# Attention on one core: sixteen 64 KB block moves a step become four of 256 KB, and the key projections read their tokens in another order

## The reference

```python
h = _layernorm(x, ln1_g, ln1_b)
x = _attention(h, h, sa_wq, sa_wk, sa_wv, sa_wo, sa_bo) + x
h = _layernorm(x, ln2_g, ln2_b)
x = _attention(h, cond_emb, ca_wq, ca_wk, ca_wv, ca_wo, ca_bo) + x
h = _layernorm(x, ln3_g, ln3_b)
p = h @ ff_w1 + ff_b1
a, gate = (p[..., :D_FF], p[..., D_FF:])
h = a * jax.nn.gelu(gate, approximate=False) @ ff_w2 + ff_b2
return h + x
```

## Time and profile before

| | |
|---|---|
| median of 3 runs | 2921.08 us (2920.36 to 2922.96) |
| the profiled execution, its own time | 2921.73 us |
| span of its trace | 2919.9 us |
| busy: PE, DVE, ACT, POOL | 2874.1, 2279.7, 1906.4, 1470.9 us |
| TensorE clock granted, mean | 0.998 |
| DMA packets | 535597, 413.62 MB |
| self-attention, cross-attention, feed-forward | up to about 1203, 2371, 2920 us |

### The profile page before, as it was taken

How to read it: one execution, slowest core, us unless ns; L and a number is a source line. 1 busy time by engine, 2 the same in 40 slices (tenths; PEclk the granted TensorE clock), 3 DMA queues, 4 the chain that set the end, 5 groups by cost and what they waited for, 6 DMA issues and landing times.

```text
span 2919.9 us, 75820 instructions
## 1 busy us (share of the span) xinstructions
PE 2874.1 (98%) x25278; PEld 2506.6 (86%) x25278; DVE 2279.7 (78%) x3495; ACT 1906.4 (65%) x6041; POOL 1470.9 (50%) x1310
## 2 busy tenths in 40 slices
PE   8999999999999999999999999999999999999999
PEld 6888888888888888877788888888888889999999
DVE  6888888888888888888888888888888865555554
ACT  6666676776666667876677777777777754444443
POOL 5444444444444444754555555555555545454454
PEclk9999999999999999999999999999999999999999
DMA  5555565555555555556666666666665532222222
GB/s 146 152 158 157 159 158 156 156 157 149 150 149 149 146 149 151 152 157 164 160 168 172 169 167 160 162 160 160 164 160 160 154 107 72 90 72 75 87 72 62
DMA packets 535597, 413.62 MB, mean 142 GB/s; under 512 B 171200, under 2 KB 520768, under 8 KB 535488
## 3 DMA queue, kind: packets, MB, share of 16 engines
q1 hardware_dynamic: 443424, 328.31, 41.4%
q10 hardware_dynamic: 92064, 83.96, 11.3%
HBM read 94.52 MB, written 49.02 MB: 49 GB/s over the span
## 4 chain that ended last, share of the span: by engine, by line
PE 59%; SPq 12%; ACT 11%; DVE 7%; issue 5%; ACTq 3%; DMA 1%; POOL 1%; DVEq 0%; POOLq 0%
PE unit_ps L594 32%; PE s_ps L594 12%; SPq L524 11%; PE o_ps L619 8%; PE s_ps L607 7%; ACT probs L851 7%; DVE neg_max L1031 2%; DVE blocks L1045 2%; ACTq L867 2%; ACT qk_hi L889 2%; DMA rows_in<-rows_t_dram 1%; DVE hT_lo L1073 1%; DVE hT_lo L1069 1%; ACT x_n L829 1%; DVE qk_lo L1056 1%
## 5 line engine op out<-in xcount | busy, mean ns | idle before, releaser
L1261 POOL TENSOR_TENSOR probs<-probs,row_inv 128x1024 f32<-128x1024 f32 x512 | 966.9, 1894 | 946.8 <-DVE row_inv L1036 946.8
L851 ACT ACTIVATE probs<-s_ps,neg_max 128x256 f32<-128x256 f32 x2048 | 950.5, 490 | 268.3 <-DVE neg_max L1031 267.9
L1031 DVE TENSOR_REDUCE neg_max<-s_ps 128x4 f32<-128x1024 f32 x512 | 615.4, 1202 | 72.2 <-PE s_ps L607 72.1
L1045 DVE STREAM_TRANSPOSE blocks<-probs 128x1024 f32<-128x1024 f32 x512 | 632.1, 1235 | 21.4 <-POOL probs L1261 21.2
L594 PE MATMUL unit_ps<-hT_hi,w_hi 128*128 128x256 f32 x2048 | 572.5, 283 | 2.8 <-DVE hT_lo L1069 2.2
L594 PE MATMUL unit_ps<-hT_hi,w_lo 128*128 128x256 f32 x2048 | 555.4, 277 | 0.0
L619 PE MATMUL o_ps<-pT,v_f 128*64 128x256 f32 x4096 | 498.5, 385 | 3.9 <-DMA pT<-blocks 2.0
L594 PE MATMUL unit_ps<-hT_lo,w_hi 128*128 128x256 f32 x1792 | 496.9, 277 | 0.0
L851 ACT ACTIVATION_READ_ACCUMULATOR probs<-s_ps,neg_max 128x1 f32 x2048 | 453.4, 221 | 0.0
L594 PE MATMUL unit_ps<-w_hi,a_hi 128*128 128x256 f32 x1536 | 438.2, 285 | 2.6 <-DVE a_lo L1051 1.5
L594 PE MATMUL unit_ps<-w_hi,a_lo 128*128 128x256 f32 x1536 | 435.0, 283 | 0.0
(11 more groups left out here) (73 smaller groups left out, 6003.6 us busy)
## 6 DMA issues: line engine op xcount, KB each, us to landing
pT<-blocks SPq DMA_DIRECT2D x3072, 64.0 KB, 2.0
pT<-blocks ACTq DMA_DIRECT2D x1024, 64.0 KB, 2.1
rows_t_dram<-row_blocks SPq DMA_DIRECT2D x91, 256.0 KB, 2.4
rows_in<-rows_t_dram SPq DMA_DIRECT2D x91, 256.0 KB, 3.0
x_res<-in_x_dram SPq DMA_DIRECT2D x32, 256.0 KB, 2.9
x_sa_dram<-x_out SPq DMA_DIRECT2D x32, 256.0 KB, 2.4
x_ln<-x_sa_dram ACTq DMA_DIRECT2D x32, 256.0 KB, 3.2
ctx_in<-in_ctx_dram SPq DMA_DIRECT2D x32, 256.0 KB, 2.9
```

The source lines that it names most:

```text
L851: op = nc.scalar.activation(probs[:, m % 2, r, :], s_ps[:, m % 2, r // IT, r % IT * S:(r % IT + 1) * S], ACT.Exp, bias=neg_max[:, m % RING ...
L1031: nc.vector.tensor_reduce(neg_max[:, m % RING, :], s_ps[:, m % 2, :, :].rearrange("p h (i j) -> p (h i) j", j=S), AX_X, ALU.max, negate=Tr ...
L1045: nc.vector.transpose(blocks[:, n % 2, m % 2, :, :].rearrange("p b (j r c) -> p r j b c", j=IT, c=BLK), probs[:, m % 2, :, :].rearrange("p ...
L1261: nc.gpsimd.tensor_tensor(probs[:, m % 2, :, :], probs[:, m % 2, :, :], row_inv[:, m % RING, :].unsqueeze(2).broadcast_to([P, ROWS, S]), A ...
```

## The change

All 16 moves of a step become four, all issued by SyncE. Move `i` takes the 32 partitions of block row `i` with all four block columns, and writes all 128 partitions of `pT`: the 8 KB of each source partition are cut into four runs of 2 KB, which go to four neighbouring partitions. The buffers' dimensions are reordered for that. Element order now puts column `j` * 32 + `c` of the probabilities on partition 4 `c` + `j`. So that this is again the partition of the right token for the values, the keys are put in another order: the key projection's moving operand is read through `by_quadrant`, 32 tokens with a step of four (16 bytes), starting at token 0, 1, 2 and 3 of each half. Its result is written to PSUM in unbroken order. Queries and values are read as before.

```diff
-MOVES = 16 * NB * NB
+MOVES = 16 * NB
...
-        blocks = sb("blocks", [P, 2, 2, NB, IT * ROWS * BLK])
-        pT = sb("pT", [P, 2, 2, NB, IT * ROWS * BLK])
+        blocks = sb("blocks", [P, 2, NB, 2, IT * ROWS * BLK])
+        pT = sb("pT", [P, 2, NB, 2, IT * ROWS * BLK])
...
                 for i in range(NB):
-                    for j in range(NB - 1 if i < pass_of(b, home).by_act else NB):
-                        sp.dma_start(pT[j * BLK:(j + 1) * BLK, n % 2, :, i, :],
-                                     blocks[i * BLK:(i + 1) * BLK, n % 2, :, j, :]).then_inc(landed(b, n, home)[0], 16)
+                    sp.dma_start(pT[:, n % 2, i, :, :], blocks[i * BLK:(i + 1) * BLK, n % 2, :, :, :]).then_inc(landed(b, n, home)[0], 16)
...
-                    p = pT[:, n % 2, i, :, :].rearrange("p a (j h i c) -> p j h i a c", j=IT, h=2, i=IT)
+                    p = pT[:, n % 2, :, i, :].rearrange("p a (j h i c) -> p j h i a c", j=IT, h=2, i=IT)
...
+            def by_quadrant(tokens):
+
+                return tokens.rearrange("p (j c b) -> p j b c", j=IT, c=BLK)
...
-                    product(bank[:, S:2 * S], projection(1, cols, ph.kv, slice(0, S))).then_inc(at.qk_full, 1)
+                    product(bank[:, S:2 * S].rearrange("p (j b c) -> p j b c", j=IT, c=BLK),
+                            [(w, by_quadrant(h)) for w, h in projection(1, cols, ph.kv, slice(0, S))]).then_inc(at.qk_full, 1)
...
-            def move_blocks(b, n, home):
-                act.wait_ge(at.blocks_done, b * PAIRS + 2 * n + 2)
-                at_least(act, at.o_full, b * STEPS + n - 1)
-                for i in range(pass_of(b, home).by_act):
-                    j = NB - 1
-                    act.dma_start(pT[j * BLK:(j + 1) * BLK, n % 2, :, i, :],
-                                  blocks[i * BLK:(i + 1) * BLK, n % 2, :, j, :]).then_inc(landed(b, n, home)[0], 16)
...
-                nc.vector.transpose(blocks[:, n % 2, m % 2, :, :].rearrange("p b (j r c) -> p r j b c", j=IT, c=BLK),
+                nc.vector.transpose(blocks[:, n % 2, :, m % 2, :].rearrange("p b (j r c) -> p r j b c", j=IT, c=BLK),
```

More of the change, by code:

```diff
@@ L271, in block_kernel, with __init__ @@
         class Pass:
-            def __init__(self, name, norm, x_in, x_to, has_ctx, weights, first, by_act):
-                self.by_act = by_act
+            def __init__(self, name, norm, x_in, x_to, has_ctx, weights, first):
                 self.norm, self.x_in, self.x_to, self.has_ctx, self.first = norm, x_in, x_to, has_ctx, first
@@ L334, in __init__ @@
                 self.y_done = sem(f"{name}_y_done")
-        sa = Pass("sa", 0, x, x_sa, False, (sa_wq, sa_wk, sa_wv, sa_wo), 0, 4)
-        ca = Pass("ca", 1, x_sa, x_ca, True, (ca_wq, ca_wk, ca_wv, ca_wo), B, 4)
+        sa = Pass("sa", 0, x, x_sa, False, (sa_wq, sa_wk, sa_wv, sa_wo), 0)
+        ca = Pass("ca", 1, x_sa, x_ca, True, (ca_wq, ca_wk, ca_wv, ca_wo), B)
         at = Attention("at")
@@ L917, in end_attention @@
                 split_ff_weight(0)
-                move_blocks(last, 3, ca)
                 split_ff_weight(1)
@@ L966, in attention_iteration @@
                         split_inputs(t + 1, home)
-                    if ready := moved(t, n, parts):
-                        move_blocks(*ready, home)
                     for p in hi_last(t, n):
```

## The result

The changed kernel takes 3220.07 us in the median (3219.23 to 3221.59, 4 runs) against 2921.24 before: a ratio of 1.1025, 95% interval 1.1011 to 1.104. It is 299 us slower. The forecast was 3223.

The account below looks back on a forecast made before the run. PE's own stream was taken as the bound nearly everywhere, with about 25 us of waits on SyncE's moves. 2921.7 + 327 - 25 = 3224, less 0.6 for the runs' median: 3223 us; 8 in 10 range 2893 to 3260.

Parts of the forecast that it names:

- What bounds the kernel: Whole kernel: PE's own stream bounds nearly everywhere; about 25 us it waits, around cross-attention, for what SyncE's move queue delays.
- The moves, -25 us: Cross-attention and its end: fewer SyncE issues remove PE's waits, -25 us (ends 0 and -27); self-attention gains zero.
- The moves' own sizes: SyncE's queue, per step: four issues 2.6 us for 7.7, landing 3.0 us, last landing after 5.6 us for 9.7.
- The packets: DMA transfers, whole program: about 404,500 packets in place of 535,597, as the moves' 262,144 become 131,072.
- The attend matmuls, 0: PE's attend: runs of 32 elements stay, only their distance doubles to 2 KB; 0, upper end 12 us.
- The key read, +327 us: Key projections on PE: reading by 16 bytes halves the pace, +0.116 us for each of 2816 matmuls, +327 us.
- The reason for it: Key projections: strided DVE and ScalarE writes cost about one more pass; a 16 byte step gives one access per line.
- A free read: Rival, key projections: PE's strided read costs nothing, only the queue's gain remains, 2896 us; chance 0.34.
- The absolute price: Rival, key projections: each matmul gains some 0.30 us, as DVE's writes do, 3746 us in all; chance 0.09.
- A partly covered read: Rival, key projections: the read runs ahead and loses only 10 to 70 ns a matmul, 2925 to 3095 us; chance 0.07.
- A queue that did not matter: Rival, cross-attention: PE was not waiting for the queue and the read is free, 2921 us; chance 0.04.

Follow-up runs that it names:

- the moves alone: The changed kernel with key projections reading tokens in natural order again, its four large moves kept: 2891.77 us against 2922.66 for the kernel before.
- the relieved queue: The kernel before, sixteen moves and natural reads kept, with residual rows and context loaded by GpSimd's queue instead of SyncE's: 2916.69 us against 2924.8.
- read alone: The kernel before, its sixteen 64 KB moves kept, with key projections reading one token in four: 3224.0 us, ratio 1.1034.
- the steps of 8 bytes: The changed kernel with the key read in two interleaved halves, step 8 bytes in place of 16: 3214.19 us, ratio 1.0998.
- the pairs: The changed kernel with the key read as two neighbouring elements, 16 bytes from pair to pair: 3214.68 us, ratio 1.0988.
- the fours off the line: The changed kernel, 248 key tokens read in runs of four starting 8 bytes late, 8 in a short matmul: 3496.1 us; unshifted control 3199.61.
- DVE's read: The changed moves with natural keys on PE; DVE's block transposes read the probabilities with a 16 byte step: 3114.09 us, ratio 1.0645.
- ScalarE's write: The changed moves, natural keys on PE and DVE; ScalarE's exponentials write probabilities in block order, elements 128 bytes apart: 3013.93 us, ratio 1.0309.
- ScalarE's read of PSUM: The changed moves, natural keys on PE and DVE; ScalarE's exponentials read scores with a 16 byte step and write straight: 2891.67 us, ratio 0.989.

## Why the prediction was right, step by step

**What bounds the kernel.** Right. PE's stream sets the time outside cross-attention: the gain of the moves alone leaves self-attention at 36.96 us, and the whole price of the read appears in the time.

**The moves, -25 us.** Right in kind and in place, somewhat undersized: -30.9 in the medians, -29.2 between the two profiled executions. Of these 29.2 us, 26.6 lie between the first scores of cross-attention and the last, 2.3 behind them and 0.3 ahead. The forecast counted PE's idle time; that fell by 20.9 us (45.8 to 24.9), and PE's busy time fell by 8.2 us too (2874.1 to 2865.9), which idle time cannot tell of. It named the load of rows_in as the link; the moves' own landing, which it saw only at the end of attention, is a part earlier too, as the relieved queue suggests. In the changed kernel the gain is covered almost wholly: read alone minus both is 3224.0 - 3220.1 = 4 us. The sum 327 - 25 is right all the same, because the slower PE takes away the same waits: put into the kernel before, the read costs 301 us and not 328.

**The moves' own sizes.** Too low. SyncE's four issues took 3.86 us for 2.6 forecast: the first two take 0.55 and 0.60 us, about as forecast, the third and fourth 1.0 and 1.5 (medians). A landing took 4.5 us for 3.0. From the first issue of a step to its last landing it is 7.4 us, where 5.6 were forecast and the kernel before takes 9.2. The landings of other loads grew as well (rows_in 3.0 to 4.1). That follows the moves and not the read: with the read alone they are 2.0 and 3.0 us, with the moves alone 4.6 and 4.2; what in four 256 KB transfers slows them was not tested. It did no harm: in the changed kernel a step's last move landed 8.7 us before its attend in self-attention and 7.2 us in cross-attention (medians).

The packets came to 355,360, not 404,500. Besides the 131,072 runs saved, there are 49,152 fewer packets under 512 B (171,200 to 122,048), which is 16 for each of the 3072 transfers fewer; the two account for all but 13 of the 180,237. The line of the kernel before:

```profile
DMA packets 535597, 413.62 MB, mean 142 GB/s; under 512 B 171200, under 2 KB 520768, under 8 KB 535488
```

**The attend matmuls, 0.** Right: 16 of them still take 1.88 us in the chain, and the batch of the moves alone is unchanged.

**The key read, +327 us.** Right: both kernels with the same moves, the changed one and the moves alone, are 3220.1 - 2891.8 = 328.3 us apart, 0.117 us for each of 2816 matmuls. By part it is 42.77 - 36.96 = 5.81 us for 48 of them in self-attention (forecast 5.6) and 4.5 for 40 in cross-attention (4.6).

**The reason for it.** Half right. The size was taken from writes by DVE and ScalarE, whose price per element is their own matter, and the estimate of one more pass compared two different DVE operations (a transpose and a normalisation). That half pace came out of it was in part luck: at 8 bytes ScalarE's write is nearly free, and PE's read at 8 bytes is as slow as at 16. Had the change used a step of 8 bytes, the same argument would have forecast a gain and been wrong by 320 us. The Trainium skill's "Advanced Engine Details and Errata", SBUF Cachelines, asks for at least two accesses to a 16 byte line; the steps of 8 bytes, the pairs and the fours off the line have two and run at half pace (0.23, 0.23 and 0.22 us), so for this read the measurement is stricter than the rule. The Trainium skill's "SBUF — State Buffer", in the note on cachelines under "Door 1: The DMA port swizzle", lets fp32 be strided by 4 for free; for this read the changed kernel itself refutes it (0.23 us in place of 0.114).

**The rivals.** A free read: refuted, the read costs 0.117 us a matmul where it had to cost under 0.009. The absolute price: refuted, nothing exceeds the doubling, even with one element used of a line's four and the next line skipped. A partly covered read (10 to 70 ns a matmul): refuted by the same 117 ns. A queue that did not matter: refuted by the moves alone.

## What to carry to other kernels

A layout that saves another engine's work is paid where its permutation is undone; put it on the access that is free, and try each candidate engine, since reads and writes of the same step differ. Here PE's read, DVE's read and ScalarE's write each turned a gain of 31 us into a loss of 299, 189 and 90, and ScalarE's read of PSUM kept it whole. For a moving operand like this one (float32r, 256 columns), keep runs that are whole 16 byte lines, beginning on one.

## What was not expected of the hardware

- PE's read of a moving operand has two paces, not a slope: a matmul of 256 columns starts every 0.114 us when each 16 byte line is used whole and every 0.22 to 0.23 when two elements or one of it are used, also when every second line is skipped (0.22).
- A matmul of 8 columns with 128 x 128 weights starts every 0.11 us, as one of 248 does. So below 256 columns something other than the columns sets the distance, perhaps the load of the weights, which no run varied. At 256 columns the slower reads showed in full.
- ScalarE reads PSUM with a step of 16 bytes at no cost (488 ns against 490), but its write of single elements 128 bytes apart takes 750 ns.
- DVE's block transpose slows from 1235 to 2045 ns when it reads by 16 bytes, which is less than a doubling.
